# Moving half of a residual add to the start of an FFN, with a third buffer for its down product and a reordered tail

## The reference, cut to what matters

```python
x = x + attn(cond_conv(x, ...), Wq, Wk, Wv, Wo, ...)          # 32 heads, 8 key/value heads
f = cond2(x, cond_128, ...)                                   # per-sample mixing of the 32 rows
# ffn: int4 weights, dequantised in groups of 128 rows: (w - zero) * scale
gate = silu(f @ deq(gate_w))                                  # 512 -> 1792
up = f @ deq(up_w)                                            # 512 -> 1792
x = x + (gate * up) @ deq(down_w)                             # 1792 -> 512, and the residual x
```

## Time and profile before

| | us |
|---|---|
| median of 3 runs | 682.78 (681.7 to 682.87) |
| the profiled execution, device time | 682.99 |
| its span, first to last instruction | 681.2 |
| PE busy in the span | 660.1 (97%) |
| DVE busy | 563.0 (83%) |
| POOL busy | 458.0 (67%) |
| ACT busy | 411.2 (60%) |
| FFN, from its first gate product to the last instruction | 500.2 to 681.2 |
| the transfers T(1) to T(24), issue to landing, median | 4.6 |

### The profile page before, as it was taken

How to read it: one execution, slowest core, us unless ns; L and a number is a source line. 1 busy time by engine, 2 the same in 40 slices (tenths; PEclk the granted TensorE clock), 3 DMA queues, 4 the chain that set the end, 5 groups by cost and what they waited for, 6 DMA issues and landing times.

```text
span 681.2 us, 14436 instructions
## 1 busy us (share of the span) xinstructions
PE 660.1 (97%) x4952; PEld 369.6 (54%) x4952; DVE 563.0 (83%) x870; ACT 411.2 (60%) x1233; POOL 458.0 (67%) x379
## 2 busy tenths in 40 slices
PE   9999999999999999999999999999989999999994
PEld 8855555656556465664656646566544444344441
DVE  4968779879879788987977978877776999899986
ACT  0477663844647374374655638447465877877773
POOL 0467974874786497287569548738537678887885
PEclk9999999999999999999999999999989999999999
DMA  7520257379468348536735944663300156656553
GB/s 252 198 93 2 69 172 145 81 209 138 117 105 259 93 95 269 113 80 172 184 106 101 265 101 84 179 82 104 52 1 1 36 109 118 111 109 139 102 105 104
DMA packets 112672, 82.70 MB, mean 121 GB/s; under 512 B 93264, under 2 KB 93936, under 8 KB 110448
## 3 DMA queue, kind: packets, MB, share of 16 engines
q1 hardware_dynamic: 108736, 69.51, 40.5%
q0 software_dynamic: 3456, 12.58, 9.9%
q10 hardware_dynamic: 432, 0.01, 0.0%
HBM read 48.14 MB, written 2.21 MB: 74 GB/s over the span
## 4 chain that ended last, share of the span: by engine, by line
PE 65%; DVE 10%; POOL 8%; issue 6%; DMA 6%; ACT 4%; SPq 0%; POOLq 0%; DVEq 0%; ACTq 0%
PE bank L672 18%; PE bank L673 18%; PE bank L674 18%; DMA acc<-dprod 5%; DVE exact L2015 3%; PE bank L726 2%; PE bank L872 2%; POOL wqlo L2139 2%; POOL whole L2267 1%; POOL whole L2272 1%; DVE acc L2037 1%; DVE part L2004 1%; PE bank L856 1%; PE bank L843 1%; PE bank L844 1%
## 5 line engine op out<-in xcount | busy, mean ns | idle before, releaser
L672 PE MATMUL bank<-wohi,oThi 128*128 128x512 f16 x256 | 97.1, 379 | 2.4 <-DVE oTlo L1786 2.3
L672 PE MATMUL bank<-wqhi,cThi 128*128 128x512 f16 x256 | 97.0, 379 | 0.8 <-POOL wqlo L2139 0.6
L674 PE MATMUL bank<-wohi,oTlo 128*128 128x512 f16 x256 | 97.0, 379 | 0.0
L673 PE MATMUL bank<-wolo,oThi 128*128 128x512 f16 x256 | 97.0, 379 | 0.0
L674 PE MATMUL bank<-wqhi,cTlo 128*128 128x512 f16 x256 | 97.0, 379 | 0.0
L673 PE MATMUL bank<-wqlo,cThi 128*128 128x512 f16 x256 | 97.0, 379 | 0.0
L1204 ACT ACTIVATE qraw<-bank 128x512 f32<-128x512 f32 x64 | 37.9, 591 | 82.5 <-PE bank L674 82.2
L2149 POOL TENSOR_TENSOR wolo<-wor,wohi 128x512 f16<-128x512 f32 x32 | 42.6, 1352 | 58.0 <-ACT wohi L1184 58.0
L2187 POOL TENSOR_TENSOR qinv<-qms,neghalf 128x8 f32<-128x8 f32 x28 | 53.5, 1912 | 39.4 <-ACT qms L1223 39.4
L1215 ACT ACTIVATE qsq<-qraw 128x128 f32<-128x128 f32 x256 | 75.5, 302 | 1.7
L2015 DVE SCALAR_TENSOR_TENSOR exact<-bank,uscl,exact 128x512 f32<-128x512 f32 x84 | 62.7, 747 | 11.4 <-ACT exact L1449 6.4
(11 more groups left out here) (231 smaller groups left out, 1808.7 us busy)
## 6 DMA issues: line engine op xcount, KB each, us to landing
acc<-dprod POOLq DMA_DIRECT2D x24, 512.0 KB, 4.6
wqr<-in_wq SPq DMA_DIRECT2D x8, 1024.0 KB, 7.4
wor<-in_wo SPq DMA_DIRECT2D x8, 1024.0 KB, 9.1
raw<-in_gu_w SPq DMA_DIRECT2D x28, 256.0 KB, 3.2
zeros<-in_gu_z SPq DMA_DIRECT2D x28, 256.0 KB, 4.6
wkvr<-in_wkv SPq DMA_DIRECT2D x8, 512.0 KB, 7.3
raw<-in_dn_w SPq DMA_DIRECT2D x14, 256.0 KB, 2.8
zeros<-in_dn_z SPq DMA_DIRECT2D x14, 256.0 KB, 3.7
```

The source lines that it names most:

```text
L672: mm(o, ahi, bhi, start=start and k == 0, stop=False)
L673: mm(o, ahi, blo, start=False, stop=False)
L674: last = mm(o, alo, bhi, start=False, stop=stop and k == n - 1)
```

## The change

1. **Residual blocks 0 and 2 of the first half.** PE transposes them at the start of the FFN (after the first and the second piece of the last output projection), ACT copies them into `acc`, and DVE's first down product is added on top (`down_added_to` loses its special case for n = 0). Blocks 1 and 3 keep their late add; they are transposed in n = 16 and n = 17, and `result(1)` and `result(3)` stand in n = 16 and n = 17.
2. **A third down buffer.** `dprod3`; ACT's block 1 of tile n waits for T(n - 3). The wait on POOL's first add in the last tile goes.
3. **The tail.** PE makes the high products of a tile first, as they wait only for the high half, and then the low ones. ACT makes the last high half ahead of `down_scaled(26, 1)`. POOL no longer waits for DVE's last low half before its second add.
4. **Bounds.** `hidden_power(0)` stands ahead of DVE's first gate additions. The last step of `hidden_diagonal` is a `scalar_tensor_tensor` in place of a `tensor_scalar` with two scalars.

```diff
+        def moved_blocks(n):
+            return dprod3 if n % 3 == 2 else dprod[:, n % 3, :, :]
...
@@ SP, stores of the first half @@
             for c in range(KC):
-                sp.wait_ge(d_res, c + 1)
+                if c % 2:
+                    sp.wait_ge(d_res, c // 2 + 1)
+                else:
+                    sp.wait_ge(d_dn, down_added(IC - 1, c))
...
@@ PE, last_downs @@
                 n = TILES - 2
+                pe.wait_ge(a_hhi, n + 1)
+                pe.wait_ge(d_res, 2)
+                down_high(n, 1)
+                pe.wait_ge(d_g, 2 * TILES)
+                down_high(n, 0)
+                pe.wait_ge(d_us, 3 * TILES - 1)
+                down_high(n, 2)
                 pe.wait_ge(p_hlo, n + 1)
-                pe.wait_ge(d_res, KC)
-                down_block(n, 1)
-                pe.wait_ge(d_g, 2 * TILES)
-                down_block(n, 0)
-                pe.wait_ge(d_us, 3 * TILES - 1)
-                down_block(n, 2)
+                down_low(n, 1)
+                down_low(n, 0)
+                down_low(n, 2)
...
@@ PE, start of the FFN and the loop @@
             project_out(UNITS - 1, 1, HKV - 1, 0)
+            turn_x(0, 0)
             gate(1)
             project_out(UNITS - 1, 1, HKV - 1, 1)
+            turn_x(0, 2)
             up(1)
+            pe.wait_ge(a_xT, 2)
...
                 elif n in (IC + LAG, IC + LAG + 1):
-                    turn_x(0, 2 * n - 2 * IC - 2 * LAG)
+                    turn_x(0, 2 * n - 2 * IC - 2 * LAG + 1)
...
-                elif n in (IC + LAG, IC + LAG + 1):
-                    turn_x(0, 2 * n - 2 * IC - 2 * LAG + 1)
...
@@ ACT @@
-                if n == TILES - 1:
-                    act.wait_ge(p_acc, 1)
-                elif n >= 3 and c == 1:
-                    act.wait_ge(l_acc, down_moved(n - 2))
+                if n >= 4 and c == 1:
+                    act.wait_ge(l_acc, down_moved(n - 3))
...
+            hidden_high(TILES - 1)
             down_scaled(TILES - 2, 1)
-            hidden_high(TILES - 1)
...
@@ DVE @@
-                V.tensor_scalar(hdiag[0:MAXIMA, :], ident[0:MAXIMA, 0:MAXIMA], hrow[0:MAXIMA, :], TOP,
-                                ALU.mult, ALU.mult).then_inc(d_hdiag, 1)
+                V.scalar_tensor_tensor(hdiag[0:MAXIMA, :], ident[0:MAXIMA, 0:MAXIMA], TOP,
+                                       hrow[0:MAXIMA, :].broadcast_to([MAXIMA, MAXIMA]), ALU.mult,
+                                       ALU.mult).then_inc(d_hdiag, 1)
...
             def result(c):
-                dve.wait_ge(t_xT, KC + c + 1)
-                if c % 2:
-                    dve.wait_ge(l_acc, down_moved(IC - 1))
-                else:
-                    dve.wait_ge(d_dn, down_added(IC - 1, c))
+                dve.wait_ge(t_xT, KC + 2 + c // 2 + 1)
+                dve.wait_ge(l_acc, down_moved(IC - 1))
...
+            hidden_power(0)
             scaled(0, 1)
             scaled(0, 3)
             outputs_low(UNITS - 1, range(3))
-            hidden_power(0)
...
                 scaled(n, 1)
-                if n in (IC + LAG + 1, IC + LAG + 2):
-                    result(2 * n - 2 * IC - 2 * LAG - 1)
                 scaled(n, 3)
...
                 if n in (IC + LAG, IC + LAG + 1):
-                    result(2 * n - 2 * IC - 2 * LAG)
+                    result(2 * n - 2 * IC - 2 * LAG + 1)
...
@@ POOL @@
             add_down(DIRECT, 1, 0)
-            pool.wait_ge(d_hlo, 1)
             add_down(TILES - 2, 1, 1)
```

More of the change, by code:

```diff
@@ L1086, in last_downs @@
                 n = TILES - 1
-                pe.wait_ge(d_hlo, 1)
[L1088 to L1094, removed]
-            def turn_x(half, c):
[L1098 to L1101, removed]
+                pe.wait_ge(a_hhi, n + 1)
+                pe.wait_ge(a_u, TILES)
+                down_high(n, 1)
+                down_high(n, 0)
+                pe.wait_ge(d_dn, down_added(n - 2, 2))
+                down_high(n, 2)
+                pe.wait_ge(d_dn, down_added(n - 2, 3))
+                down_high(n, 3)
+                pe.wait_ge(d_hlo, 1)
+                for c in (1, 0, 2, 3):
+                    down_low(n, c)
+            def turn_x(half, c):
+                if half:
+                    pe.wait_ge(a_xT, 2 + c)
+                    if c == 0:
+                        pe.wait_ge(d_y, HQ * UNITS)
+                        pe.wait_ge(a_hm, 2)
+                elif c % 2:
+                    pe.wait_ge(a_xT, 2 + KC)
+                    if c == 3:
+                        pe.wait_ge(d_res, 1)
                 elif c:
-                    pe.wait_ge(a_xT, c)
+                    pe.wait_ge(a_xT, 1)
                 else:
-                    pe.wait_ge(d_y, HQ * UNITS)
-                    pe.wait_ge(a_hm, 2)
+                    pe.wait_ge(a_hm, 1)
                 for t in range(HQ):
@@ L1462, in down_scaled, with turned_x @@
                 act.wait_ge(t_dn, down_done(n, c))
-                if n == TILES - 1:
-                    act.wait_ge(p_acc, 1)
-                elif n >= 3 and c == 1:
-                    act.wait_ge(l_acc, down_moved(n - 2))
-                A(dprod[:, n % 2, c // 2, :] if n else acc[:, 0, place(c), :], down_bank(n, c)[:, :], ACT.Copy,
+                if n >= 4 and c == 1:
+                    act.wait_ge(l_acc, down_moved(n - 3))
+                A(moved_blocks(n)[:, c // 2, :] if n else acc[:, 0, place(c), :], down_bank(n, c)[:, :], ACT.Copy,
                   scale=dsc[:, half, i, c:c + 1]).then_inc(a_dn, 1)
-            def turned_x(c):
-                act.wait_ge(t_xT, c + 1)
-                A(acc[:, 1, place(c), :], side[:, :], ACT.Copy).then_inc(a_xT, 1)
+            def turned_x(half, c):
+                act.wait_ge(t_xT, c + 3 if half else c // 2 + 1)
+                A(acc[:, half, place(c), :], side[:, :], ACT.Copy).then_inc(a_xT, 1)
             mix_out(1)
@@ L2027, in down_added_to @@
                 dve.wait_ge(t_dn, down_done(n, c))
[L2028 to L2040 removed]
+                if c == 3 and n == DIRECT:
+                    dve.wait_ge(l_acc, down_moved(n))
+                elif c == 3:
+                    dve.wait_ge(p_acc, 3)
+                elif i:
+                    dve.wait_ge(d_dn, down_added(n - 1, c))
+                else:
+                    dve.wait_ge(a_xT, c + 3 if half else c // 2 + 1)
+                V.scalar_tensor_tensor(o, down_bank(n, c)[:, :], dsc[:, half, i, c:c + 1], o, ALU.mult,
+                                       ALU.add).then_inc(d_dn, 1)
             def hidden_low(n):
```

35 lines of the change are left out of this document (15 added, 20 removed).

## The result

The changed kernel takes 687.78 us (median of 4 runs, 686.86 to 688.2), the kernel before 682.64 in the same session: ratio 1.0063, 95% interval 1.004 to 1.0086, so 2.7 to 5.9 us slower. The direction is that of the forecast; the loss is larger. The median lies 2.2 us above the 685.6 forecast and above the end of the range, 687.0.

A forecast was written before the change was run, and what follows sets the result against it. PE was taken to bound the FFN, with DVE only just not the bound. Terms +3.3 - 0.6 + 0 - 0.55 - 0.55 = +1.6 us, with the clock +2.8 us, gave 685.6 us; range 682.0 to 687.0 us.

The forecast's parts named there:

- The stall: n = 16: DVE reaches result(1) 3.7 us before T(13) lands; PE gap 3.25 us, cost 3.65 us.
- the 0.4 us more that I had for group 2: gate(17), behind PE's gap: group 2 waits for the next up_added, 0.8 against PE's 0.43 us; 0.4 us more.
- My upper bound of 4.9 us: n = 16: DVE's wait is at most 4.9 us, with T(13) as long as T(8), 5.99 us.
- The clock: Behind PE's new gap the clock more likely than not falls to its lower level; +1.2 us, bounds 0 and +1.65.
- My bound of 1.65 us: Behind PE's new gap: 3.5 us at clock 0.53 instead of 1.00 lose at most 1.65 us.
- Bound ahead: FFN start: hidden_power(0) moved into DVE idle time removes PE's two gaps in gate(1); -0.6 us, bounds 0 and -0.6.
- The bound of half 1: hdiag near 548 us: as scalar_tensor_tensor it still waits for POOL's instruction; 0 us, other end -0.7.
- Residual blocks: FFN start, n = 16 and 17: moved transposes net 0; a PE gap behind a DVE addition goes, gain 0.35 us.
- Third buffer: Between 560 and 591 us: ACT's transfer waits go, POOL's limit next; -0.55 us, bounds 0 and -1.9, end no earlier.
- Tail: After T(24) lands: POOL's four additions run back to back, 1.40 us each; -0.55 us, bounds -0.3 and -1.1.
- PE never makes time good: Behind the wait in n = 16: PE is full from there on, so lost time is not recovered.
- the one for more than one loss: Rival: the stall makes T(14) and first-half stores collide, or the clock falls twice; +1.5 us, 687.1 us, chance 0.06.

The follow-up runs named there:

- filled kernel: Changed kernel with the first product pair of gate(17) made thirteen times, 5.2 us of matmuls in place of PE's idle gap; 686.14 us, ratio 1.0058.
- c1_no_move: Kernel before plus third buffer, hidden_power(0) moved ahead and new tail, with residual blocks and hdiag as they were; 682.1 us, ratio 0.9992.
- t1_tail: Kernel before with only the new order of the last two tiles; 682.76 us, ratio 0.9996.
- c2_no_move_diag: As c1_no_move, with hidden_diagonal(1) behind DVE's first scaling of tile 6, last step still a tensor_scalar; 680.88 us, ratio 0.997 against the kernel before.
- p1_after_pad: Changed kernel with 24 already satisfied waits added to PE ahead of its first real work; 687.88 us, ratio 1.0072 against the kernel before.
- before: The kernel before the change, unedited; 682.64 us in the changed kernel's session.
- b1_third_buffer: Kernel before with only the third down buffer added; 682.18 us, ratio 0.9991.

## Why the prediction was right in direction and short in size

- **The stall: mechanism right, size wrong.** This is the step that failed, "T(13) is issued by POOL only in n = 16 itself, at 606.61, and lands 4.57 us later". The landing was right, the issue was not: it hung on T(12), which I had at its 4.5 us. DVE waited 5.64 us instead of 3.7. PE's gap was 5.27 us instead of 3.25; the 0.4 us more that I had for group 2 did not come on top of the slow matmuls, so +1.6 us. My upper bound of 4.9 us let only T(13) be long, though the earlier trace rows showed that a long transfer delays the issue of the next. Over the kernels with this placement the wait follows T(12) one to one: 5.2 us gave 4.2, 5.3 gave 4.3, 6.7 gave 5.6 to 5.7. Carried on to 4.5 us, which no run of this placement had, that is 3.5.
- **The clock: right.** It fell, for 3.4 us, at 0.58 in the row, and cost 1.4 us where I had taken 1.2. The filled kernel confirms it. My bound of 1.65 us was too low: with 24 waits the same gap cost 2.4 us.
- **Bound ahead: right.** From `gate(1)` to `gate(2)` -0.19 us. Four of the moved transposes, 0.44 us, are in there, so -0.63 against -0.6. Without the transposes (`c1_no_move`) the stretch takes 11.22 us, -0.63 as well.
- **The bound of half 1: right.** `hdiag` as a `scalar_tensor_tensor` takes what it took, and PE's gap is the same:

```profile
548.15 0.92 DVE L2003 SCALAR_TENSOR_TENSOR hdiag<-const,hrow 4x4 f32<-4x4 f32 x1
```

  It starts 0.80 us into POOL's 1.71 us at 547.35 and ends with it. The lock that the Trainium skill ("SBUF — State Buffer", section "SBUF: two separate sides") describes agrees.
- **Residual blocks: right.** The transposes only changed place; the 0.35 us gap went and is in the 12.32 us (6.44 + 5.27 + 1.42 - 0.44 - 0.35 = 12.34).
- **Third buffer: the place was wrong, and the gain depends on the transfers.** I had -0.55 us between 560 and 591 and nothing at the end. Alone, the buffer did put PE 0.5 us ahead by `gate(13)`, but waits for POOL's `hT` took it back by `gate(15)`, and the trace's gain of 0.8 us comes behind `gate(27)`, where I had said that the end does not come earlier. By its ratio it is -0.6 us (-1.4 to +0.2), which does not exclude nothing. In the changed kernel `gate(2)` to `gate(17)` is 0.10 us longer than before instead of 1.0 shorter (0.44 of them the transposes moved ahead). The seven other kernels with the same order of work up to there took between 2.2 us less and 0.8 us more than the changed one's 88.84, not all with the same transfers long; so one trace cannot give a size of 0.5 us here.
- **Tail: half of it.** By trace the tail alone gave 0.25 us and 0.28 us in the changed kernel, against 0.55. The mis-sized term is the spacing of POOL's additions, which I took as 1.40 us from start to start for all. Three of the four take 1.27 us, as before, and one 1.54 (minimum, median and maximum in ns, then the row of DVE beside it):

```profile
L2321 POOL TENSOR_TENSOR acc<-acc,dprod x4: 1265/1266/1535, 677.4 to 681.9; 128x512 f32<-128x512 f32 x4
```

```profile
678.06 1.19 DVE L2068 TENSOR_TENSOR hT<-whole,hT 128x512 f16<-128x512 f32 x1
```

  The long one is the second, which starts at 678.85 beside DVE's last low half; the removed wait had kept these two apart. It is 1.54 us in the traces of `t1_tail`, `c1_no_move` and `c2_no_move_diag` too. That they wait for each other at the ports is my reading; no run tested it.
- **"PE never makes time good" was too strong ahead of n = 16.** T(5), 6.4 us in the changed kernel against 5.6, put PE 1.3 us behind at n = 11, and it was level again at n = 14. Gains are lost there in the same way, as the third buffer's was. From n = 17 to `gate(27)` it did hold: nothing came back.

By stretches, the 2.4 us between the +2.8 of the forecast and the +5.2 of the trace are -0.4 to `gate(1)` (the clock's fall in the trace of before), +1.1 from `gate(2)` to `gate(17)` (the third buffer's gain, which did not come, and a long T(5)), +1.8 in the iteration of the stall (+1.6 the stall, +0.2 the clock) and -0.1 behind `gate(18)`. The first of these is luck: without it the trace would stand 2.8 us above the forecast. Of the rivals, the one for more than one loss had the size (687.1) by another road: neither the stores nor a second fall of the clock, but a longer transfer ahead of the one waited for.

## What to carry to other kernels

Before a wait is moved forward on an engine, find what issues the awaited thing and when; if transfers are chained, bound the wait with the longest of the transfer before as well, and do not put an engine with no slack behind the chain. If the matrix engine stops for several us by it, add the slow clock behind the gap. A small instruction that waits for POOL's running one, as `hdiag` did, is better moved, with one that POOL does not delay (here the scaling of a PSUM bank) ahead of it, than written as another operation. And before a difference of half a microsecond is read from two traces, compare a stretch that the change does not touch.

## What the runs showed of the hardware that I had not expected

- A transfer of 512 KB within SBUF that takes 4.5 us takes 6.7 to 6.9 in 14 of the 27 cases in which a fetch of 16 KB of instructions begins 4.5 to 5.2 us after its issue, and in no other of 336. Changes far away in the program select which transfer it is: T(12) in the changed kernel and four of its variants, T(3), T(4), T(7), T(9), T(17) or T(22) in others. Run by run the kernels with ten executions spread over 3.2 to 5.0 us; that the fetches cause this too is a guess, since one execution of each was traced.
- Waits that are long satisfied are not free on PE: 96 of them left it idle for 1.59 us and put L690 2.57 us later; 24 put nothing later, L690 starting at 8.20 us against 8.54.
- Gaps of 4.1 to 5.2 us lowered TensorE's clock to between 0.50 and 0.58 over the next 3.5 us; gaps of 1.0 and 1.3 us with four matmuls between did not. The same gap cost 1.4 us in the changed kernel's trace and 2.4 in that of `p1_after_pad`. At the start of the FFN, where three kernels run the same code, the clock fell in `before` and stayed up in `b1_third_buffer` and `t1_tail`; over all it fell there in four of the fourteen traces.
